# A three-layer edge network on one core: two gather pairs fewer, narrower node ranges, and nodes turned by the transposing form of the product

## The chip, the cores and the metric

The kernel runs on one core of a Trainium2 chip. The metric is the device time in microseconds of one execution; lower is better. TensorE (PE in the views), its weight loads (PEld), VectorE (DVE), ScalarE (ACT), GpSimd (POOL) and SyncE (SP) run side by side and meet at semaphores; 16 DMA engines move data.

## The reference

3125 nodes with 128 features, 53125 edges with 64 attributes, sorted by target `dst`. Three layers, then a last normalisation of `x` plus the result:

```python
for k in range(3):
    e = edge_vector @ edge_W[k] + edge_b[k]
    msg = relu(x[src] + e)
    agg = segment_sum(msg, dst, num_segments=n)
    z = (1.0 + eps[k]) * x + agg
    h = relu(batch_norm(z @ W1[k] + b1[k]))
    x = relu(layer_norm(h @ W2[k] + b2[k], ln_g, ln_b))
```

## The kernel before

**Bodies.** The edges are cut into 26 blocks of 2048 (16 tiles of 128 edges). Two blocks make a body, so there are 13 bodies, and each layer goes through all 13: 39 visits. A block is worked in four quads of four tiles. The first block of a body is called s, the second p.

**Two ways to fetch x[src].** The p block's rows come by indirect DMA: GpSimd issues four of them for each quad (`gather` of the gpsimd part, line 634), into `rows`. For quad q of the next body it waits until VectorE has added the rows of the present one (`p_added`). The s block is sorted by the remainder class of its source before the layers begin, so that each of its tiles needs only a few of 25 "slices" of the node table. `FIRST[t]` is the first slice that tile t may need and `SPAN[t]` how many. TensorE selects the rows (`gather`, lines 1499 to 1511): for each tile and slice, called a pair here, three bfloat16 products, one for each part of the table (x split in three, in `xs` and `xr`), with a one-hot matrix `hot_g` in float8 as weights. 68 pairs make 204 products a body, in quads of 48, 57, 54 and 45. The one-hots stand in `hot_g` by `RUNS`, 36 pairs for the first half of the tiles and 35 for the second; layer 0 builds them on VectorE (`build_hots`) and ScalarE (`last_hots`) and stores them, the later layers load them.

**Sum and scatter.** VectorE adds the gathered rows and the edge term: `add_s` (line 1167, from PSUM, waits for the gather's `g_filled`) and `add_p` (line 1174), in turns, one quad at a time. ScalarE applies the relu and widens the one-hots of the targets (`widen`, lines 731 and 733). TensorE then adds the messages into a PSUM bank by float32 products: `scatter_s` (line 1525) over `SORT_WINDOW` = 144 node columns that begin at the body's first target, `scatter_p` (line 1536) over `WINDOW` = 64 columns that begin at the quad's first target. Four products each a quad; the hardware records two weight loads and two products for each float32 product.

**Nodes.** From the third body on, each body also works two node tiles of 121 nodes of the layer's dense part: `transposed` (line 1545) turns the scaled x by a float32 product with the identity, then `hidden` (1552) and `output` (1558, 1560), with VectorE and ScalarE steps in between. The last four tiles come at the end of a layer.

**Staging.** Before the layers, 52 quads of edge attributes are multiplied by the weights of all three layers (lines 1491 and 1493), biased (1071), copied, scattered in sorted order and stored; VectorE also makes the targets' one-hots there (`hots_of`, line 1089), `HOT_COLS` = 416 words a quad, that is 104 KB, which every visit loads again (line 491).

**A branch for other data.** Before all this VectorE compares the edges with the windows and spans (`misfits`); edges that don't fit take a general loop, the `Else` branches.

**Order.** Each engine has its program written out by hand. In one visit TensorE runs: the turning of two node tiles, gather of quad 2, scatter of quad 0, gather 3, hidden, scatter 1, gather 0 of the next body, output, scatter 2, gather 1 of the next body, scatter 3.

Of the kernel before, what the change touches and what calls it, by code (L numbers as in the profile page):

```python
# [19 lines left out]
NODE_TILE = -(-NODES // BLOCKS)  # L20
NODE_TILES = BLOCKS
NODES_PAD = NODE_TILES * NODE_TILE
SORT_WINDOW = 144
WINDOW = 64
OVERLAP = BANK_COLS - NODE_TILE
GROUP = BANK_COLS // FEAT
GROUPS = -(-NODE_TILES // GROUP)
# [7 lines left out]
HALF = BLOCK_TILES // 2  # L35

FIRST = (0, 1, 2, 3, 5, 6, 8, 9, 11, 13, 14, 16, 17, 19, 21, 22)
SPAN = (3, 4, 4, 5, 4, 5, 5, 5, 5, 4, 5, 4, 5, 4, 3, 3)
SPANS = max(SPAN)

RUNS = (((0, 8), (0, 8), (0, 8), (1, 8), (3, 8)), ((8, 16), (8, 16), (8, 16), (8, 14), (8, 13)))
PAIRS_OF = [sum(b - a for a, b in runs) for runs in RUNS]
PAIRS = max(PAIRS_OF)
CHUNKS = ((0, 8), (8, 14), (14, SLICES))
# [2 lines left out]
SRT_COLS = LAYERS * FEAT + 2  # L47
HOT_COLS = QUAD * (SORT_WINDOW + WINDOW) // 2
EARLY_NODES = 20
# [20 lines left out]
def node(l, t):  # L70

    return l * NODE_TILES + t + 1


def pair_at(t, k):

    runs = RUNS[t // HALF]
    return sum(b - a for a, b in runs[:k]) + t - runs[k][0]


def constants():
# [5 lines left out]
    for s in range(SLICES):  # L87
        held = [t for t in range(BLOCK_TILES) if FIRST[t] <= s < FIRST[t] + SPAN[t]]
        c[:, C_LOW + s] = held[0] * P
# [6 lines left out]
def build(nc, x, attr, src, dst, dst_first, tabs, edge_w, edge_b, vecs, w1, w2, b2, ln_g, ln_b, tables, srt, ep, relrow, kept, hotrow, out):  # L96
# [3 lines left out]
    NT = NODE_TILE  # L100

    with ExitStack() as ctx:
        def sb(name, shape, dt=f32):
            return ctx.enter_context(nc.sbuf_tensor(name, shape, dt))

        def sem(name):
            return ctx.enter_context(nc.semaphore(name))
# [53 lines left out]
        ident = sb("ident", [P, P])  # L161
# [41 lines left out]
        relB = sb("relB", [P, 2, 2, HALF * P], f16)  # L203
        hot_s = sb("hot_s", [P, 2, QUAD * SORT_WINDOW])
        hot_p = sb("hot_p", [P, 2, QUAD * WINDOW])
        hot_stage = sb("hot_stage", [P, BLOCK_QUADS, HOT_COLS], bf16)
# [11 lines left out]
        def node_buffer(n):  # L218

            at = hot_words + n * TAIL * FEAT  # L220
            return region[:, at:at + TAIL * FEAT].rearrange("p (h d) -> p h d", h=TAIL)

        x_first = later[0:NT, 2 * QUAD * FEAT:2 * QUAD * FEAT + 4 * FEAT].rearrange("p (s h d) -> p s h d", s=2, h=2)
        x_eps, norm = node_buffer(0)[0:NT], node_buffer(1)[0:NT]
# [42 lines left out]
        def x_part(part, s):  # L267

            words = xr if part == 1 else xs
            return words[0:SLICE, :].bitcast(bf16)[:, 2 * s * FEAT + (part < 2):2 * (s + 1) * FEAT:2]  # L270
# [69 lines left out]
        xT_ready = sem("xT_ready")  # L340
# [39 lines left out]
        def wait_alone(eng, name, semaphore, value):  # L380

            eng.wait_ge(semaphore, value)
            eng.sem_inc(waits_passed[name], 1)
# [298 lines left out]
        def _(act):  # L682
# [43 lines left out]
            def widen(l, j, q):  # L726
# [3 lines left out]
                wait_alone(act, "act", s_done, l * LAYER_QUADS + j * BLOCK_QUADS + (q + BLOCK_QUADS - 1))  # L730
                nc.scalar.activation(hot_s[:, q % 2, :], packed[:, 0:QUAD * SORT_WINDOW], ACT.Copy).then_inc(hs_ready, 1)
                wait_alone(act, "act", p_done, l * LAYER_QUADS + j * BLOCK_QUADS + (q + BLOCK_QUADS - 1))
                nc.scalar.activation(hot_p[:, q % 2, :], packed[:, QUAD * SORT_WINDOW:], ACT.Copy).then_inc(hp_ready, 1)

# [5 lines left out]
            def last_hots(j, h):  # L740
# [9 lines left out]
                k = SPANS - 1  # L750
                a, b = RUNS[h][k]
                at, n = pair_at(a, k) * P, (b - a) * P
# [157 lines left out]
        def _(dve):  # L910
# [112 lines left out]
            for n, (limit, compare) in enumerate((  # L1023
                    (SORT_WINDOW, ALU.is_ge), (WINDOW, ALU.is_ge), (0, ALU.is_lt), (BANK_COLS - SORT_WINDOW, ALU.is_gt),
                    (BANK_COLS - WINDOW, ALU.is_gt), (0, ALU.is_lt), (0, ALU.is_lt), (0, ALU.is_gt))):
                ins = nc.vector.tensor_scalar(misfits[:, n:n + 1], ends[:, n:n + 1], float(limit), None, compare)
# [50 lines left out]
            def hots_of(g, first=0, stop=BLOCK_QUADS):  # L1077
# [5 lines left out]
                for at, window, relative in (  # L1083
                        (0, SORT_WINDOW, meta_s[:, g * BLOCK_TILES:(g + 1) * BLOCK_TILES, 1]),
                        (QUAD * SORT_WINDOW, WINDOW,
                         dst_rel[:, (2 * g + 1) * BLOCK_TILES:(2 * g + 2) * BLOCK_TILES])):
# [52 lines left out]
            def build_hots(j, h, first=0, stop=SPANS):  # L1139
# [9 lines left out]
                for k in range(first, stop):  # L1149
                    a, b = RUNS[h][k]  # L1150
                    at = pair_at(a, k) * P
# [314 lines left out]
        def _(pe):  # L1466
            for t in range(BLOCK_TILES):
                if t % QUAD == 0:
                    pe.wait_ge(one_ready, t // QUAD + 1)
                for b, weights in enumerate((tri, ones_b)):  # L1470
                    ins = nc.tensor.matmul(bank(b, BODIES * SLICES).rearrange("p (g s) -> p g s", s=SLICES), weights[:, :],
                                           one_s[:, t::BLOCK_TILES, :], start=t == 0, stop=t == BLOCK_TILES - 1,
                                           skip_group_check=True)
# [3 lines left out]
                             stop=True).then_inc(misfit_sum, 1)  # L1477
# [20 lines left out]
            def gather(l, j, q):  # L1498
# [6 lines left out]
                for t in range(q * QUAD, (q + 1) * QUAD):  # L1505
                    c = (t % QUAD) * FEAT
                    for k in range(SPAN[t]):
                        at = pair_at(t, k) * P
                        for part in range(3):
                            ins = nc.tensor.matmul(bank(q)[:, c:c + FEAT], hot_g[v % 2][0:SLICE, h, at:at + P],  # L1510
                                                   x_part(part, FIRST[t] + k), start=k == 0 and part == 0,
                                                   stop=k == SPAN[t] - 1 and part == 2, skip_group_check=True)
                ins.then_inc(g_filled, 1)
# [16 lines left out]
            def scatter_p(l, j, q, col):  # L1530
# [4 lines left out]
                for t in range(QUAD):  # L1535
                    ins = nc.tensor.matmul(ps[:, bass.ds(col, WINDOW)],  # L1536
                                           terms[:, BLOCK_QUADS + q, t * FEAT:(t + 1) * FEAT],
# [4 lines left out]
            def transposed(l, t, h, zh=zh_cols):  # L1542

                pe.wait_ge(x_eps_ready, node(l, t))
                nc.tensor.matmul(zh(h, 0), x_eps[:, h, :], ident[0:NT, 0:NT],  # L1545
                                 start=True, stop=True, skip_group_check=True).then_inc(xT_ready, 1)

            def hidden(l, t, h, upto, zh=zh_cols):

# [19 lines left out]
            def body(l, j):  # L1569
# [11 lines left out]
                if nodes:  # L1581
                    transposed(l, *a)
                    transposed(l, *b)
# [21 lines left out]
                if not last:  # L1605
                    gather(l, j + 1, 1)
                else:
                    pe.wait_ge(s_added, (l + 1) * LAYER_QUADS + BLOCK_QUADS)
                    for h in range(TAIL):
                        transposed(l, first + h, h, tail_zh)  # L1610
# [28 lines left out]
            with pe.Else():  # L1639
                pe.wait_ge(tables_ready, 1)  # L1640
                with pe.Fori(0, LAYERS) as l:

                    pe.wait_ge(x_eps_ready, l + 1)
                    for g, ts in enumerate(groups()):
                        for t in range(ts.start, ts.stop):
                            c = g * BANK_COLS + (t - ts.start) * NT
                            nc.tensor.matmul(ps[:, c:c + NT], result[:, t, :], ident[0:NT, 0:NT],
                                             start=t == ts.start, stop=False, skip_group_check=True)
                    with pe.Fori(0, BLOCKS) as b:
                        for k in range(BLOCK_QUADS):  # L1650
# [3 lines left out]
                            for j in range(QUAD):  # L1654
                                nc.tensor.matmul(bank(7)[:, j * FEAT:(j + 1) * FEAT], ones_b[0:B2_PARTS, :],
                                                 b2_split[:, bass.ds(l + LAYERS, 1), :].rearrange("p a d -> p (a d)"),
                                                 start=True, stop=False, skip_group_check=True)
                                ins = nc.tensor.matmul(bank(7)[:, j * FEAT:(j + 1) * FEAT],
                                                       g_attr[0:EDGE_FEAT, k, j * P:(j + 1) * P], one(we, l),
                                                       start=False, stop=True, skip_group_check=True)  # L1660
                            ins.then_inc(gg_filled, 1)
                            pe.wait_ge(g_msg, q + 1)
                            for j in range(QUAD):
                                for g in range(GROUPS):
                                    pe.wait_ge(g_hot, (q * QUAD + j) * GROUPS + (g + 1))
                                    nc.tensor.matmul(bank(g, GROUP_COLS), g_msgs[:, k % 2, j * FEAT:(j + 1) * FEAT],
                                                     onehot_all, start=False, stop=False,
                                                     skip_group_check=True).then_inc(g_used, 1)
# [5 lines left out]
                    for g, ts in enumerate(groups()):  # L1674
                        n = (ts.stop - ts.start) * NT
                        ins = nc.tensor.matmul(bank(g, n), w1_cur[:, :], zT_all[:, g * GROUP_COLS:g * GROUP_COLS + n],
                                               start=True, stop=True, skip_group_check=True)
                    ins.then_inc(g_step, 1)
                    wait_alone(pe, "pe", g_step, at + 3)
                    for g, ts in enumerate(groups()):  # L1680
# [3 lines left out]
                                         start=True, stop=False, skip_group_check=True)  # L1684
                        for t in range(ts.start, ts.stop):
                            c = g * BANK_COLS + (t - ts.start) * FEAT
                            ins = nc.tensor.matmul(ps[0:NT, c:c + FEAT], hT_all[:, t * NT:(t + 1) * NT], one(w2_all, l),
                                                   start=False, stop=t == ts.stop - 1, skip_group_check=True)
# [58 lines left out]
```

## Time and profile before

| | us |
|---|---|
| median of 3 runs | 1580.73 (1569.49 to 1582.17) |
| profiled execution, its own time | 1595.68 |
| its span, first to last instruction | 1593.9 |
| mean granted TensorE clock (1 is 2.4 GHz) | 0.862 |
| staging, to the first gather on TensorE | about 335 |
| three layers and the last normalisation | about 1259 |

The profiled execution is 15 us, or 0.9%, over the median. Busy shares of the span: PE 75%, PEld 65%, DVE 45%, ACT 35%, POOL 53%. A time of a row is the start in us from the span's beginning; "busy" of a group is the union of its instructions' times, while the mean of one is its own latency, and matmuls overlap: the step from one start to the next is what a further product costs. "issue" as a releaser stands for idle time whose end nothing in the trace explains; "remote" in the views of this single core is a semaphore whose sender the trace doesn't find.

### The profile page before, as it was taken

To read this page: it belongs to the slowest core of one execution; us is meant where nothing else is said; L and a number is where in the kernel's file an instruction comes from. 1 tells how busy PE (TensorE), PEld (TensorE's weight loads), DVE (VectorE), ACT (ScalarE), POOL (GpSimd) and SP (SyncE) were. 2 spreads that over 40 slices of the span, in tenths; PEclk is the share of its full clock that TensorE was granted. 3 is DMA by queue.
4 is the path that set the end of the run, shared out by engine and by line. 5 is a ranking of instruction groups with operands and counts; after the bars stand their busy time and mean duration, and the time that the engine had idled before them with its cause. 6 is when DMAs were issued, how large, how long until landed. Compare 5 with 4: busy or idle time off the path is not lost.

```text
span 1593.9 us, 31830 instructions
## 1 busy us (share of the span) xinstructions
PE 1200.5 (75%) x11868; PEld 1030.8 (65%) x11868; DVE 719.3 (45%) x1546; ACT 551.4 (35%) x1146; POOL 839.7 (53%) x842
## 2 busy tenths in 40 slices
PE   4666656666888878886588888788856888888886
PEld 2333323355778778776477877777845777787776
DVE  7576456564454454455122333233351244344345
ACT  1223323233444444442233333333422333333333
POOL 6777667756555454432555545544155445445440
PEclk8879888787988898987798998889967899988987
DMA  9999999995565656556355555555634555555541
GB/s 240 324 320 352 298 337 344 325 297 174 177 184 169 183 166 184 179 178 195 88 174 144 169 170 156 165 150 158 186 100 139 173 162 152 175 160 166 171 136 52
DMA packets 252723, 309.79 MB, mean 194 GB/s; under 512 B 53005, under 2 KB 169791, under 8 KB 252583
## 3 DMA queue, kind: packets, MB, share of 16 engines
q1 hardware_dynamic: 208734, 218.79, 44.8%
q0 software_dynamic: 33280, 82.06, 16.2%
q10 hardware_dynamic: 10569, 6.97, 1.9%
q8 instruction: 100, 1.64, 0.4%
q14 instruction: 40, 0.33, 0.1%
HBM read 200.17 MB, written 107.55 MB: 193 GB/s over the span
## 4 chain that ended last, share of the span: by engine, by line
PE 64%; issue 19%; DVE 8%; another core or an unknown queue 5%; DMA 2%; ACT 1%; SPq 1%; DVEq 0%; ACTq 0%
PE ps L1510 33%; PE ps L1525 11%; PE ps L1536 9%; PE ps L1491 5%; DVE terms L1071 2%; PE ps L1560 2%; DMA ep_dram<-terms 2%; PE ps L1545 1%; PE ps L1552 1%; PE ps L1558 1%; DVE hot_stage L1089 1%; PE ps L1493 1%; ACT region L711 1%; DMA attr_x<-attr_dram 1%
## 5 line engine op out<-in xcount | busy, mean ns | idle before, releaser
L634 POOL DMA_INDIRECT rows<-table_dram,src_i x416 | 402.1, 967 | 440.2 <-DVE terms L1174 256.2
L1167 DVE TENSOR_TENSOR terms<-ps,terms 128x512 f32<-128x512 f32 x156 | 107.8, 691 | 667.3 <-PE ps L1510 333.5
L1510 PE MATMUL ps<-xs,early_words 125*128 125x128 bf16 x2720 | 292.1, 230 | 82.2 <-issue 73.0
L1510 PE MATMUL ps<-xs,region 125*128 125x128 bf16 x2584 | 271.1, 230 | 53.2 <-issue 52.9
L634 POOL DMA_INDIRECT rows<-x_dram,src_i x208 | 211.9, 1019 | 175.4 <-DVE terms L1174 121.4
L1510 PEld LDWEIGHTS ps<-xs,early_words 125*128 125x128 fp8e4 x2720 | 231.8, 103 | 99.0 <-issue 89.2
L1510 PE MATMUL ps<-xr,early_words 125*128 125x128 bf16 x1360 | 265.2, 230 | 35.5 <-issue 35.2
L1491 PE MATMUL ps<-wf,attr_x 64*128 64x384 f32 x416 | 187.5, 603 | 112.9 <-issue 61.5
L654 POOL DMA_INDIRECT srt_dram<-region,pos_i x208 | 223.5, 1075 | 88.8 <-issue 59.1
L1510 PE MATMUL ps<-xr,region 125*128 125x128 bf16 x1292 | 250.7, 230 | 17.3 <-issue 17.2
L1510 PEld LDWEIGHTS ps<-xs,region 125*128 125x128 fp8e4 x2584 | 220.7, 103 | 59.7 <-issue 59.5
L1525 PE MATMUL ps<-hot_s,terms 128*128 128x144 f32 x1248 | 213.4, 316 | 21.0 <-issue 19.0
L1491 PEld LDWEIGHTS ps<-wf,attr_x 64*128 64x128 f32 x416 | 91.3, 232 | 196.4 <-issue 170.6
L718 ACT ACTIVATE terms<-terms 128x512 f32<-128x512 f32 x156 | 97.6, 625 | 340.2 <-DVE terms L1167 304.2
L1525 PEld LDWEIGHTS ps<-hot_s,terms 128*128 128x128 f32 x1248 | 185.5, 212 | 30.9 <-issue 30.6
L1536 PE MATMUL ps<-hot_p,terms 128*128 128x64 f32 x1248 | 178.2, 284 | 23.8 <-issue 22.8
L1536 PEld LDWEIGHTS ps<-hot_p,terms 128*128 128x128 f32 x1248 | 170.2, 206 | 34.7 <-issue 34.2
L1493 PE MATMUL ps<-wf,attr_x 64*128 64x384 f32 x416 | 188.8, 606 | 0.0
L1510 PEld LDWEIGHTS ps<-xr,early_words 125*128 125x128 fp8e4 x1360 | 138.5, 102 | 46.0 <-issue 45.7
L711 ACT ACTIVATE region<-ps 128x768 f32<-128x768 f32 x104 | 84.0, 811 | 214.4 <-PE ps L1491 86.5
L1071 DVE TENSOR_TENSOR terms<-ps,eb_all 128x768 f32<-128x768 f32 x104 | 96.9, 953 | 125.7 <-remote 38.9
L1510 PEld LDWEIGHTS ps<-xr,region 125*128 125x128 fp8e4 x1292 | 132.3, 102 | 25.8 <-issue 25.2
(129 smaller groups left out, 1315.8 us busy)
## 6 DMA issues: line engine op xcount, KB each, us to landing
ep_dram<-terms SPq DMA_DIRECT2D x52, 768.0 KB
terms<-srt_dram SPq DMA_DIRECT2D x156, 256.0 KB
terms<-ep_dram SPq DMA_DIRECT2D x156, 256.0 KB
early_words<-hotrow_dram SPq DMA_DIRECT2D x156, 104.0 KB
attr_x<-attr_dram SPq DMA_DIRECT2D x52, 256.0 KB
region<-kept_dram SPq DMA_DIRECT2D x13, 576.0 KB
early_words<-kept_dram SPq DMA_DIRECT2D x13, 576.0 KB
region<-kept_dram SPq DMA_DIRECT2D x13, 560.0 KB
```

What stands on the lines that cost most here:

```text
L634: pool.indirect_dma_start(rows[:, q, t * FEAT:(t + 1) * FEAT], None, source, bass.IndirectOffsetOnAxis(ap=src_i[:, c:c + 1], axis=0),).the ...
L654: pool.indirect_dma_start(srt, bass.IndirectOffsetOnAxis(ap=pos_i[:, c:c + 1], axis=0), stage_s[:, q, t, :], None).then_inc(scattered[q], 16)
L711: nc.scalar.activation(stage_s[:, q, tiles, 0:LAYERS * FEAT], ps[:, 0:QUAD * BANK_COLS].rearrange("p (t c) -> p t c", t=QUAD) [:, tiles, 0 ...
L718: nc.scalar.activation(terms[:, q, :], terms[:, q, :], ACT.Relu).then_inc(s_relu, 1)
L1071: nc.vector.tensor_tensor(stage_p[:, n % 2, :].rearrange("p (l t d) -> p t l d", l=LAYERS, t=QUAD)[:, tiles], ps[:, BLOCK_QUADS * BANK_COL ...
L1167: nc.vector.tensor_tensor(terms[:, q, :], bank(q), terms[:, q, :], ALU.add).then_inc(s_added, 1)
L1491: of_s = nc.tensor.matmul(bank(t, width), attr_x[0:EDGE_FEAT, slot, cut], wf[0:EDGE_FEAT, :], start=True, stop=True, skip_group_check=True)
L1493: of_p = nc.tensor.matmul(bank(BLOCK_QUADS + t, width), attr_x[EDGE_FEAT:P, slot, cut], wf[EDGE_FEAT:P, :], start=True, stop=True, skip_gr ...
L1510: ins = nc.tensor.matmul(bank(q)[:, c:c + FEAT], hot_g[v % 2][0:SLICE, h, at:at + P], x_part(part, FIRST[t] + k), start=k == 0 and part == ...
L1525: ins = nc.tensor.matmul(ps[:, bass.ds(col, SORT_WINDOW)], terms[:, q, t * FEAT:(t + 1) * FEAT], hot_s[:, q % 2, t * SORT_WINDOW:(t + 1) * ...
L1536: ins = nc.tensor.matmul(ps[:, bass.ds(col, WINDOW)], terms[:, BLOCK_QUADS + q, t * FEAT:(t + 1) * FEAT], hot_p[:, q % 2, t * WINDOW:(t + ...
L1560: nc.tensor.matmul(y(h), hT[:, h, :], w2_all[:, l, :], start=False, stop=True, skip_group_check=True).then_inc(y_ready, 1)
```

## The change

Four constants and one call. Tile 1 loses its fourth slice and tile 6 its fifth; the pair of tile 1 also goes from the stored one-hots (36 to 35 pairs), that of tile 6 stays stored and isn't used. The target windows shrink from 144 to 132 and from 64 to 48 columns, and with them `HOT_COLS` from 416 to 360. The two nodes' turning uses the engine's transposing form.

```diff
-SORT_WINDOW = 144
-WINDOW = 64
+SORT_WINDOW = 132
+WINDOW = 48
...
-SPAN = (3, 4, 4, 5, 4, 5, 5, 5, 5, 4, 5, 4, 5, 4, 3, 3)
+SPAN = (3, 3, 4, 5, 4, 5, 4, 5, 5, 4, 5, 4, 5, 4, 3, 3)
...
-RUNS = (((0, 8), (0, 8), (0, 8), (1, 8), (3, 8)), ((8, 16), (8, 16), (8, 16), (8, 14), (8, 13)))
+RUNS = (((0, 8), (0, 8), (0, 8), (2, 8), (3, 8)), ((8, 16), (8, 16), (8, 16), (8, 14), (8, 13)))
...
             def transposed(l, t, h, zh=zh_cols):
 
                 pe.wait_ge(x_eps_ready, node(l, t))
-                nc.tensor.matmul(zh(h, 0), x_eps[:, h, :], ident[0:NT, 0:NT],
-                                 start=True, stop=True, skip_group_check=True).then_inc(xT_ready, 1)
+                nc.tensor.transpose(zh(h, 0), x_eps[:, h, :], ident[0:NT, 0:NT]).then_inc(xT_ready, 1)
```

On TensorE, where a visit of layer 0 ends with the scatter of quad 3 and the next begins by turning two node tiles (`region` holds them; `col_i` is the window's column), the program had:

```order
L1525 MATMUL ps<-hot_s,terms 128x144 x4
L1576 TENSOR_LOAD col_i
L1576 ISA x2
L1536 ISA
L1536 MATMUL ps<-hot_p,terms 128x64 x4
L1545 MATMUL ps<-ident,region 128x121 x2
```

In the changed kernel the same place reads:

```order
L1525 MATMUL ps<-hot_s,terms 128x132 x4
L1575 TENSOR_LOAD col_i
L1575 ISA x2
L1536 ISA
L1536 MATMUL ps<-hot_p,terms 128x48 x4
L1545 MATMUL ps<-ident,region 128x121 x2
```

Nothing moved there: the same instructions stand in the same order, with fewer columns. The gathers between such places are 6 products shorter a body (quad 0 from 48 to 45, quad 1 from 57 to 54), 234 in all.

On VectorE, in the staging, the one-hots of the targets (`hot_stage`) are made between the bias additions (`terms`). A piece of the difference:

```order
-L1089 TENSOR_TENSOR hot_stage<-iota_f,meta_s 128x576
-L1089 TENSOR_TENSOR hot_stage<-iota_f,dst_rel 128x256
+L1089 TENSOR_TENSOR hot_stage<-iota_f,meta_s 128x528
+L1089 TENSOR_TENSOR hot_stage<-iota_f,dst_rel 128x192
 L1071 TENSOR_TENSOR terms<-ps,eb_all 128x2x3x128 x2
```

Again only the sizes differ. VectorE has 1537 instructions in its program before and after.

## Rows read from the trace of the kernel before

**Rows 1.** The page: granted TensorE clock in 40 slices, in tenths.
```profile
PEclk8879888787988898987798998889967899988987
```
**Rows 2.** Stretch: us, busy PE, PEld, DVE, ACT, POOL, PEclk, DMA share, GB/s.
```profile
0.00:335.00 335.00, 196.31 (x871) 108.97 (x872) 203.82 (x276) 91.20 (x159) 239.95 (x233) 0.83 0.97 319
335.00:1594.00 1259.00, 1004.23 (x11000) 921.85 (x10997) 515.43 (x1271) 460.15 (x987) 599.80 (x610) 0.87 0.55 161
```
**Rows 3.** The chain that ended last, 335 to 1594 us, shares by line.
```profile
by line: PE ps L1510 41.2%; issue 19.6%; PE ps L1525 13.9%; PE ps L1536 11.3%; another core or an unknown queue 2.8%; PE ps L1560 2.7%; PE ps L1545 1.8%; PE ps L1552 1.5%; PE ps L1558 1.2%; DVE terms L1174 0.4%; DVE region L1213 0.3%; DVE s
```
**Rows 4.** Timeline of PE at 2.4 GHz: start, us, line, tiles, count.
```profile
905.58 1.15 PE L1525 MATMUL ps<-hot_s,terms 128*128 128x144 f32 x8
906.57 1.00 PE L1536 MATMUL ps<-hot_p,terms 128*128 128x64 f32 x8
907.41 0.22 PE L1510 MATMUL ps<-xs,early_words 125*128 125x128 bf16 x1
907.47 0.22 PE L1510 MATMUL ps<-xr,early_words 125*128 125x128 bf16 x1
...
926.49 0.66 PE L1545 MATMUL ps<-ident,region 121*128 121x121 f32 x4
926.98 0.22 PE L1510 MATMUL ps<-xs,early_words 125*128 125x128 bf16 x1
```
**Rows 5.** Timeline of PE at 1.2 GHz, two places.
```profile
904.81 0.31 PE L1510 MATMUL ps<-xr,region 125*128 125x128 bf16 x1
904.92 0.31 PE L1510 MATMUL ps<-xs,region 125*128 125x128 bf16 x1
...
977.28 2.12 PE L1525 MATMUL ps<-hot_s,terms 128*128 128x144 f32 x8
979.20 1.50 PE L1536 MATMUL ps<-hot_p,terms 128*128 128x64 f32 x8
```
**Rows 6.** PE inside one gather, idle time and its releaser in brackets.
```profile
914.99 0.22 PE L1510 MATMUL ps<-xr,early_words 125*128 125x128 bf16 x1 [0.52 <-issue]
916.40 0.22 PE L1510 MATMUL ps<-xs,early_words 125*128 125x128 bf16 x1 [1.19 <-issue]
```
**Rows 7.** Who waited for whom, from 335 us: total, times, longest.
```profile
PE ps L1510 <- issue: 178.3, 255, 12.1
POOL rows L634 <- DVE terms L1174: 377.6, 115, 8.6
DVE terms L1167 <- PE ps L1510: 333.5, 71, 17.4
DVE terms L1167 <- remote: 330.9, 71, 13.0
```
**Rows 8.** Timeline of POOL, one burst of four issues and the next's first.
```profile
1000.38 0.94 POOL L634 DMA_INDIRECT rows<-table_dram,src_i  x1 [2.66 <-DVE terms L1174]
...
1004.12 0.94 POOL L634 DMA_INDIRECT rows<-table_dram,src_i  x1 [0.30 <-issue]
1007.65 0.94 POOL L634 DMA_INDIRECT rows<-table_dram,src_i  x1 [2.59 <-DVE terms L1174]
```
**Rows 9.** Timeline of DVE around the same burst.
```profile
1006.09 0.69 DVE L1167 TENSOR_TENSOR terms<-ps,terms 128x512 f32<-128x512 f32 x1 [5.98 <-remote]
1006.70 0.68 DVE L1174 TENSOR_TENSOR terms<-rows,terms 128x512 f32<-128x512 f32 x1
```
**Rows 10.** Busy time by stretch: a single burst, a double one, two layer ends.
```profile
1000.38:1007.65 7.27, 6.89 (x91) 6.39 (x88) 1.50 (x3) 1.33 (x3) 3.77 (x4) 1.00 0.41 123
...
1022.30:1037.10 14.80, 9.66 (x92) 8.15 (x90) 2.73 (x5) 4.17 (x9) 7.60 (x9) 0.81 0.55 158
...
702.60:744.80 42.20, 32.96 (x314) 29.93 (x313) 20.91 (x68) 17.72 (x45) 0.03 (x1) 0.82 0.71 217
1545.00:1582.50 37.50, 34.52 (x312) 31.40 (x311) 21.41 (x74) 15.19 (x38) 0.00 (x0) 0.82 0.22 58
```
**Rows 11.** The chain in the staging, 25 to 335 us, shares by line.
```profile
by line: PE ps L1491 26.2%; issue 16.9%; another core or an unknown queue 12.7%; DVE terms L1071 11.5%; DMA ep_dram<-terms 8.1%; DVE hot_stage L1089 4.4%; PE ps L1493 3.2%; ACT region L711 2.9%; DMA attr_x<-attr_dram 2.9%; SPq L461 2.0%; DV
```

## The prediction

> **What bounds the kernel now.** I read the busy time by stretch first. Staging takes 335 us with the DMA engines 97% busy; the layers take 1259 us with PE busy for 1004, POOL for 600 and DMA 55% [rows 2]. Almost all that the change touches is in the layers, on PE. The chain of waits says the same: 41.2% of the 1259 us lies on the gather (L1510), 13.9% on scatter_s (L1525), 11.3% on scatter_p (L1536), 1.8% on the turning (L1545), and 19.6% is "issue", idle time that nothing explains [rows 3]. On that view alone PE is the bound and each PE nanosecond saved counts.
>
> The timeline speaks against taking that whole. Inside a gather, where no product waits for a semaphore, PE runs one product and stops for 0.52 or 1.19 us [rows 6]; in the gathers such and other "issue" idling sums to 178 us in 255 pieces [rows 7]. I laid these stops beside POOL. GpSimd issues its indirect DMAs in bursts of four: 0.94 us each, about 1.25 apart, so 1000.38 to 1005.06. VectorE's next add_s starts at 1006.09, a microsecond behind the burst, add_p at 1006.70, and the next burst at 1007.65 [rows 8, 9]. In steady stretches this repeats every 7.3 us: a burst of 4.7 us and 2.6 us between. Within a burst PE gets through some 50 to 60 products, and stops until about 0.9 us after its end; the semaphores that PE should have raised arrive then too, which is why half of VectorE's waits for the gather are put down to "remote" (330.9 us beside 333.5) [rows 7]. So there is a loop POOL burst, PE's late signal, add_s, add_p, POOL burst, whose period holds little that the change shortens. In one period PE started 91 products [rows 10]; a quad needs 70 (204 gather, 64 scatter and 14 node products, over four). So PE gets ahead, VectorE then adds two quads at once, and a burst of eight follows in which PE manages 92 products in 14.8 us [rows 10] and falls behind again. Of POOL's waits for VectorE, 115 with 377.6 us together [rows 7], 115 times 2.6 = 299 us is the loop's own minimum, and the other 79 us is time in which PE really is late.
>
> **The change part by part.** The sum is made against the profiled execution (span 1593.9, own time 1595.68), which is 15 us over the median of 1580.73; I take the difference over to the median unchanged.
>
> *Gather.* 39 visits times 6 products = 234 of 7956 go. A product more costs 0.06 us at 2.4 GHz (907.41 to 907.47) [rows 4] and 0.11 at 1.2 GHz (904.81 to 904.92) [rows 5]. The chain has 0.412 x 1259 / 7956 = 65 ns for one, a mix of both clocks: 234 x 65 ns = 15 us. Bounds: 13 us with no slow stretch among them, 25 with nothing else. The Trainium skill, "TensorE: Matmul & The Clock Gate", section "Back-to-back issue gap", gives about 81 ns for a weight load and product of 128 columns in a stream; by it this term would be an estimated 19 us. The trace has 57, and the row decides.
>
> *scatter_s, 144 to 132 columns.* Eight recorded products take 0.99 us at 2.4 GHz (905.58 to 906.57), 124 ns each [rows 4], and 1.92 us at 1.2 GHz, 240 each [rows 5]: exactly two passes of 144 columns at 1.2 GHz. Two passes of 132 are 10 ns shorter at 2.4 and 20 at 1.2 GHz; with a mean clock of 0.87, 1248 products give 14 us. Below, the saving could be cut off where the weight load sets the step; the rows of scatter_p put that at 105 ns, under the 114 that I expect. Bounds 4 us (a straight line from 64 columns and 105 ns to 144 and 124) and 15 us (13.9% of 1259, times 12/144).
>
> *scatter_p, 64 to 48 columns.* Eight take 0.84 us (906.57 to 907.41), 105 ns each; four products of the turning, of 121 columns, take 0.49 us, 122 each [rows 4]. Nearly twice the columns for 17 ns more: at these widths the weights of 128 columns, not the moving columns, set the step. So nothing is gained. Bounds: 0, and if it did go with the columns 11.3% of 1259 times 16/64 = 36 us, which the comparison all but excludes.
>
> *Turning.* 78 products, each four-way split now into two weight loads and two products: 0.49 us for two of them, 0.245 each [rows 4]. No transposing form is in this trace. Bounds: nothing gained (the same two passes), or 0.245 down to one bfloat16 step of 0.06, 14 us for all. I take one recorded pair in place of two, 0.12 us, 9 us in all, because the operand's width stays 4 bytes.
>
> *Not on the path.* The widening on ScalarE and the one-hot loads shrink by 13%; ScalarE is busy for 460 of 1259 us and DMA 55% [rows 2], so PE's gather in between hides them. If that cover were gone they would gain, not cost. Nothing is added, no wait is new. That the narrower windows fit follows from the reference's edges: the farthest target is 124 columns from its body's first (under 132) and 33 from its quad's (under 48), and the general branch isn't taken.
>
> *Staging.* VectorE's one-hots are 4.4% of the chain of 310 us [rows 11], 13.6 us, and lose 13.5% of their elements: 2 us.
>
> *The sum.* PE saves 15 + 14 + 0 + 9 = 38 us if it always is the path. The three layer ends, after POOL's last burst, hold about 950 of the 11000 products (314 and 312 in the two shown [rows 10]), 9%: there 3.5 us count in full. Of the other 34.5 us I count half. For it speaks that PE, once behind in a double burst, has to catch up through several quads, so that its savings add up until the next wait; against it that 299 of 378 us of POOL's waits are the loop's minimum. So 3.5 + 17 + 2 = 23 us. Span 1571, profiled 1573, median **1558 us**, 1.4% faster.
>
> **The rivals.**
>
> 1. *PE is the bound throughout.* The chain's shares speak for it. Then all 38 us count, the stops shrink with the number of products (2.9% of 178 us, 5 us), and staging 2: 45 us, 1536 us. The loop's regular 7.3 us speak against it.
>
> 2. *POOL's loop absorbs it.* PE gets earlier to a stop that ends with the burst anyway. Then the layer ends and staging are left, 5.5 us, and a little of the 79 us: 5 to 12 us, 1572 us. For it: 299 of the 378 us in which POOL waits are not due to PE being late. Against it: every double burst shows PE behind for two to three quads.
>
> 3. *The clock takes it back; slower.* PEclk falls in nearly every slice [rows 1], and 1 - 0.862, doubled, of 1594 us is 440 us at 1.2 GHz. It falls after stretches in which PE stands: the double burst has 0.81, the single one 1.00 [rows 10]. Shorter work between the same bursts means longer standing. A microsecond more at 1.2 GHz costs half a microsecond of PE work, and half of that on the path. The gain of 23 us is gone once 92 us more are spent there, a fifth over now; at a third over (147 us, 37 us lost) the time is 1595 us. Since only some 1 us in 30 a visit is freed, I hold that unlikely. The Trainium skill has a rule against the turning here (the same page, Part 4, "PE-mode transpose"): transposing products don't count as work for the clock. No row of before has one. By it the quiet time would grow by a quarter of a microsecond twice in a visit, in 33 of the visits.
>
> 4. *The turning gains nothing and scatter_s takes its lower bound.* PE saves 15 + 4, half of it counts: 12 to 13 us, 1568 us.
>
> **How the numbers follow.** Forecast 0.42 (1548 to 1567), rival 1 0.16 (1530 to 1548), rival 2 0.26 (1567 to 1578), rival 3 0.08 (1581 to 1600), rival 4 0.08. From 1536 to 1580 I leave out rival 3 and half of rival 1: about 2 in 10. About 1% is what a measurement of this kernel can tell from no change (its three runs span 0.8%), so faster is below 1565 and slower above 1597. Faster: rival 1 with most of the forecast and a part of rival 4, 0.53. Slower: the far half of rival 3 and what I haven't seen, 0.07. The rest, 0.40, is within 1%.
>
> **What would show it.** The gather has 7722 products, the scatters 1248 each; at 2.4 GHz eight of scatter_s take 0.91 us, eight of scatter_p still 0.84. If these go down to 0.63, the weights didn't set the step. The turning has 78 recorded products, not 156. POOL's steady period stays at 7.3 us; if it stays and the total of POOL's waits for VectorE falls from 378 by some 20 us, the forecast's halving is right; if those waits hardly move, rival 2. A mean clock under 0.84 speaks for rival 3. The staging ends 2 us sooner. Wrong altogether I would be if the stops in the gathers change in kind, since their cause is not known: they are 178 us, far more than all that is saved.

## The result, and the profile after

The changed kernel takes 1589.05 us (median of 20 runs, 1573.84 to 1603.92), the kernel before beside it 1581.05 (20 runs, 1569.49 to 1596.3): ratio 1.0044, 95% interval 1.0022 to 1.0065. It is 7 us slower, within 1% of before; forecast were 23 us less. A second comparison, side by side with others on one chip, gave 1.0055 (1.0020 to 1.0091). A third, on a chip where the kernel before itself takes only 1223 us, gave 0.9812 (0.9777 to 0.9847), 23 us less. The explanation needs both kinds of chip. Ratios leave out runs more than 1.5% above the fastest of their kernel; in the second comparison that is 14 of before's 29, and the plain medians there (1600.84 and 1597.78) give 1.0019, so that slowdown is known only as 0.2 to 0.6%.

TensorE's rows came out as the sum had them. Timeline of PE in the changed kernel, at 2.4 GHz, then at 1.2, then the turning (start, us, line, tiles, count), beside [rows 4, 5]:

```profile
556.97 1.07 PE L1525 MATMUL ps<-hot_s,terms 128*128 128x132 f32 x8
557.88 0.99 PE L1536 MATMUL ps<-hot_p,terms 128*128 128x48 f32 x8
558.70 0.22 PE L1510 MATMUL ps<-xs,region 125*128 125x128 bf16 x1
...
436.50 1.96 PE L1525 MATMUL ps<-hot_s,terms 128*128 128x132 f32 x8
438.26 1.13 PE L1536 MATMUL ps<-hot_p,terms 128*128 128x48 f32 x8
...
595.66 0.39 PE L1545 MATMUL ps<-ident,region 121*128 121x121 f32 x2
595.89 0.22 PE L1510 MATMUL ps<-xs,early_words 125*128 125x128 bf16 x1
```

Eight products of scatter_s take 0.91 us in place of 0.99 and 1.76 at 1.2 GHz in place of 1.92; eight of scatter_p 0.82 in place of 0.84; two turnings, now one recorded product each, 0.23 in place of 0.49. What changed elsewhere shows in the busy time by stretch (us, busy PE, PEld, DVE, ACT, POOL, PEclk, DMA share, GB/s), to be read beside [rows 2]:

```profile
0.00:335.00 335.00, 207.08 (x876) 111.19 (x877) 199.54 (x276) 90.62 (x160) 236.68 (x231) 0.78 0.95 315
335.00:1579.00 1244.00, 984.27 (x10683) 903.84 (x10680) 512.26 (x1271) 444.50 (x987) 599.68 (x611) 0.85 0.55 161
```

PEclk is lower in both stretches, 0.78 for 0.83 and 0.85 for 0.87; over 20 runs the mean granted clock is 0.837 (standard error 0.001), where before has 0.858 to 0.862 in the comparisons below that take as long. The staging's fall isn't the change's doing as far as this shows: PE's work there is the same, and the profiles of the experiments on such chips have anything from 0.79 to 0.84 there. It makes up about a third of the gap between these two profiles (0.832 for 0.862), which is why the clocks below are means over many runs. The waits of the layers, beside [rows 7] (total, times, longest):

```profile
POOL rows L634 <- DVE terms L1174: 383.1, 116, 8.0
...
DVE terms L1167 <- PE ps L1510: 396.1, 85, 17.7
...
DVE terms L1167 <- remote: 252.1, 57, 9.5
...
PE ps L1510 <- issue: 179.8, 259, 12.0
```

POOL waits 383 us for VectorE, as before (378); PE stops for 180 us inside the gathers, as before (178). The profiled execution happens to be one of the shortest of the 20 (1580.81), so its span is no measure of the change.

### The profile page after: what moved, and what is told of

Read it like the earlier page. It is cut to its first block, busy times and chain, and to the rows that moved or that the text cites. A ratio compares the mean times of both kernels' runs of the same rounds, so it can differ in the third digit from the quotient of the medians.

```text
span 1579.0 us, 31206 instructions
## 1 busy us (share of the span) xinstructions
PE 1191.3 (75%) x11556; PEld 1015.0 (64%) x11556; DVE 711.8 (45%) x1546; ACT 535.1 (34%) x1146; POOL 836.4 (53%) x842
## 4 chain that ended last, share of the span: by engine, by line
PE 66%; issue 19%; DVE 7%; DMA 4%; another core or an unknown queue 2%; SPq 1%; ACT 0%; ACTq 0%; DVEq 0%
PE ps L1510 34%; PE ps L1525 11%; PE ps L1536 10%; PE ps L1491 6%; DMA ep_dram<-terms 4%; DVE terms L1071 2%; PE ps L1559 2%; PE ps L1551 1%; PE ps L1557 1%; PE ps L1493 1%; PE ps L1545 1%; DVE hot_stage L1089 0%; DVE xr L947 0%; DVE z_sum L993 0%
## 5 line engine op out<-in xcount | busy, mean ns | idle before, releaser
L1510 PE MATMUL ps<-xs,early_words 125*128 125x128 bf16 x2640 | 287.1, 233 | 69.2 <-issue 65.5
L1491 PE MATMUL ps<-wf,attr_x 64*128 64x384 f32 x416 | 197.2, 626 | 108.1 <-issue 57.4
L1525 PE MATMUL ps<-hot_s,terms 128*128 128x132 f32 x1248 | 204.4, 308 | 29.6 <-issue 28.2
L1525 PEld LDWEIGHTS ps<-hot_s,terms 128*128 128x128 f32 x1248 | 177.9, 213 | 43.1 <-issue 42.5
L1536 PE MATMUL ps<-hot_p,terms 128*128 128x48 f32 x1248 | 183.2, 289 | 26.8 <-issue 24.8
L1493 PE MATMUL ps<-wf,attr_x 64*128 64x384 f32 x416 | 198.6, 630 | 0.0
L1536 PEld LDWEIGHTS ps<-hot_p,terms 128*128 128x128 f32 x1248 | 177.0, 215 | 33.4 <-issue 32.2
```

Of the source, the lines that this page charges most:

```text
L1491: of_s = nc.tensor.matmul(bank(t, width), attr_x[0:EDGE_FEAT, slot, cut], wf[0:EDGE_FEAT, :], start=True, stop=True, skip_group_check=True)
L1493: of_p = nc.tensor.matmul(bank(BLOCK_QUADS + t, width), attr_x[EDGE_FEAT:P, slot, cut], wf[EDGE_FEAT:P, :], start=True, stop=True, skip_gr ...
L1525: ins = nc.tensor.matmul(ps[:, bass.ds(col, SORT_WINDOW)], terms[:, q, t * FEAT:(t + 1) * FEAT], hot_s[:, q % 2, t * SORT_WINDOW:(t + 1) * ...
L1536: ins = nc.tensor.matmul(ps[:, bass.ds(col, WINDOW)], terms[:, BLOCK_QUADS + q, t * FEAT:(t + 1) * FEAT], hot_p[:, q % 2, t * WINDOW:(t + ...
```

## The experiments

Each ratio is to the kernel before, run beside it on the same chip; the clocks are means over the runs of each kernel. The expectations name the accounts that were set against each other: theory A, that the clock follows what PE streams while it is occupied, and the rivals B to F.

### One part at a time

Four kernels, each the kernel before with one edit of the change: `SPAN` and `RUNS`; the transposing form; and

```diff
-WINDOW = 64
+WINDOW = 48
```

```diff
-SORT_WINDOW = 144
+SORT_WINDOW = 132
```

Pairs: 

> Only the two gather pairs are left out: 234 products fewer, windows and turning as before. The changed kernel took a mean granted clock of 0.832 where before had 0.862. Theory A (the clock falls because products stream fewer columns in steps that do not get shorter; here columns and steps go together): clock within 0.005 of before, time 5 to 12 us less (ratio 0.993 to 0.997). Rival B (any shortening of PE's work lengthens its standing behind GpSimd's bursts, and that lowers the clock): clock 0.85 or less, time within 3 us of before.

Turning: 

> Only the turning uses the transposing form: 78 recorded products in place of 156. Theory A: the transposed products stream less in the same place; a small fall of the clock, 0.855 or so, time within 3 us. Rival C (transposing products do not count for the clock, and they are what lowers it in the changed kernel): clock 0.84 or less, time 5 to 15 us more. Rival B: no change that can be seen, since only some 9 us of PE's work go.

scatter_p: 

> Only scatter_p's range goes from 64 to 48 columns. In the changed kernel eight of its products still take what they took before, so the engine is occupied as long and streams a quarter less. Theory A: clock 0.845 or less, time 8 to 16 us more (ratio 1.005 to 1.010). Rival B: nothing gets shorter, so clock 0.86 and time within 3 us of before.

scatter_s: 

> Only scatter_s's range goes from 144 to 132 columns; its step falls from 124 to 113 ns with it. Theory A: columns and time go together, clock within 0.006 of before, time 3 to 8 us less. Rival B: 14 us of PE's work go, PE stands that much longer, clock 0.85, time as before.

| alone | ratio (95%) | clock, before 0.858 |
|---|---|---|
| pairs left out | 1.0003 (0.9967 to 1.0039) | 0.850 |
| turning | 0.9961 (0.9933 to 0.9989) | 0.857 |
| scatter_p 48 | 1.0035 (1.0009 to 1.0060) | 0.850 |
| scatter_s 132 | 1.0010 (0.9982 to 1.0038) | 0.852 |

(Standard errors of the clocks 0.001 to 0.002, 12 runs each, 35 of before.) Theory A was right on the direction of scatter_p: it occupies PE as long, streams a quarter less, the clock falls and the kernel gets slower. The size was smaller than it wanted (0.850 for 0.845 or less, 0.35% for 0.5 to 1%). On the pairs and scatter_s it wanted a clock within 0.005 and 0.006 of before, and both fell further, by 0.008 and 0.007. Those two save 15 and 14 us of PE's work and show no gain clear of the noise. That is what rival B said of them, that PE's longer standing lowers the clock, and no run here parts it from the fewer columns in these two; but it has no account of scatter_p, which shortens nothing. Rival C falls: the turning is the one edit with a gain clear of the noise, and its clock is unchanged. The four falls sum to 0.024, and the changed kernel lies 0.02 to 0.03 under before.

### Giving columns back

The changed kernel with 64 columns in scatter_p, and the kernel before with 96 (`WINDOW = 64` and `WINDOW = 96`).

> The changed kernel with scatter_p's range put back to 64 columns. So far, apart: pairs -1.7 us with the clock 0.008 lower, scatter_s +2.1 us and 0.007 lower, turning -5.0 us and 0.001 lower, scatter_p +5.9 us and 0.008 lower than before's 0.858. If the parts add up (theory A, the clock follows what the array streams): clock 0.842, time 5 us less than before (ratio 0.997), that is 6 us under the changed kernel. Rival (the parts do not add; the changed kernel is slow by something they do only together): clock about 0.837 and ratio 1.003 or more as in the changed kernel.

Measured 0.9951 (0.9917 to 0.9984), 1573.71 us beside 1585.14, clock 0.855 (before 0.862). **This kernel is faster than before, and by its ratio faster than the changed one.** Alone 48 columns cost 0.35%; in company of the others about 0.9%.

> Kernel before with scatter_p's range widened to 96 columns: 80 thousand more column passes of products, whose step should stay at 105 ns since two passes of 96 columns are 80 ns at 2.4 GHz; the one-hot loads grow from 104 to 120 KB a quad. Theory A: clock up by 0.012 to 0.018, to 0.872, and time down by 8 to 12 us (ratio 0.993 to 0.995), the reverse of the narrower range. Rival D (the narrower range costs time for another reason than the clock, or more columns only cost): clock unchanged, time equal or up to 10 us more from larger loads.

Measured 1.0008 (0.9978 to 1.0039), clock 0.869: up by 0.006, less than expected, and no time gained. The loads and the widening also grew, so this run doesn't say whether they ate the gain or the higher clock brought none.

To part the streamed columns from the one-hots' size, the changed kernel kept its 48 columns in every store, load and widening, and only the products streamed more, over zeros set once. From the edit (ScalarE also writes its 48 columns into places 64 or 96 apart):

```diff
-        hot_p = sb("hot_p", [P, 2, QUAD * WINDOW])
+        hot_p = sb("hot_p", [P, 2, QUAD * STREAM])
...
-                    ins = nc.tensor.matmul(ps[:, bass.ds(col, WINDOW)],
+                    ins = nc.tensor.matmul(ps[:, bass.ds(col, STREAM)],
```

> The changed kernel itself once more, as the yardstick for the three beside it on one chip: ratio 1.002 to 1.007, clock 0.02 under before.

> The changed kernel, scatter_p's one-hots made, stored, loaded and widened with 48 columns, but each product streams 64: the 16 further columns of hot_p were set to zero once and add nothing. With true 64-column one-hots the kernel was 0.5% faster than before, with 48 it is 0.4% slower. Theory A (what counts is how many columns the products stream, by way of the clock): clock up by 0.01 to 0.02 over the changed kernel and ratio to before 0.993 to 0.998, as with true 64 columns. Rival F (the narrower one-hots cost by their loads, their layout or ScalarE's widening): clock and ratio as in the changed kernel, 1.002 or more.

> The same with 96 columns streamed, 48 of them zero. Eight products still take 0.84 us at 2.4 GHz, since two passes of 96 columns are 80 ns and the step is 105. Theory A: clock up once more, 0.005 to 0.015 over the stream of 64, time equal to that or up to 5 us less. In the kernel before, true 96 columns raised the clock by 0.006 and left the time as it was, so the gain may already be used up at 64. Rival F: as the changed kernel.

| on one chip, before 1597.78 us | median us | ratio (95%) | clock, before 0.859 |
|---|---|---|---|
| changed kernel | 1600.84 | 1.0055 (1.0020 to 1.0091) | 0.830 |
| 48, 64 streamed | 1585.03 | 0.9959 (0.9926 to 0.9993) | 0.848 |
| 48, 96 streamed | 1587.88 | 0.9984 (0.9946 to 1.0022) | 0.858 |

Streaming 16 columns of zeros makes the kernel 16 us faster. That shows it: the loads, the stored layout and ScalarE's work are the changed kernel's (rival F; ScalarE's widening of `hot_p` takes 356 and 355 ns), the order of instructions too, and only what the array streams differs. The profiled executions show by what way. The layers' stretch and the wait inside the gathers, first with 48 streamed, then with 64:

```profile
337.00:1609.00 1272.00, 1013.11 (x10688) 932.76 (x10688) 513.68 (x1272) 445.79 (x987) 597.37 (x610) 0.83 0.54 157
PE ps L1510 <- issue: 174.3, 246, 12.7
...
343.00:1594.00 1251.00, 975.21 (x10688) 892.81 (x10686) 513.57 (x1272) 445.62 (x987) 599.12 (x612) 0.86 0.55 160
PE ps L1513 <- issue: 185.8, 253, 13.0
```

PE has as many products and is busy for 38 us less at the higher clock, while its stops are no shorter (186 us for 174). In these two executions the time comes by the clock and not by the stops. At 96 the clock is before's and no further time comes; beyond 64 it bought nothing here.

### What GpSimd's bursts take

GpSimd issues one indirect DMA a quad after the first visit, not four. The rows of three tiles in four stay as they were, so VectorE adds old values, and its wait counts the fewer landings; all else runs. The edit takes away the issues together with their transfers.

```diff
             def gather(l, source, j, q):
 
-                for t in range(QUAD):
+                for t in range(QUAD if (l, j) == (0, 0) else 1):
```

> Kernel before, but GpSimd issues one indirect DMA a quad in place of four, except for the first visit: the rows of the other three tiles of a quad are not fetched again and stay as they were. Bursts of 1 us in place of 5. Theory of the forecast (PE's stops inside gathers come from GpSimd's bursts): the 178 us of 'issue' in the gathers fall under 60, and the time falls by 150 to 350 us. Rival E (the stops are PE's own, of its instruction supply or clock): 'issue' in the gathers stays at 150 or more and the time falls by less than 60 us.

> The changed kernel with the same cut on GpSimd (one indirect DMA a quad in place of four, the other rows stay as they were). Theory of the forecast (the loop of bursts absorbed the savings): now PE is the bound, so this is 35 to 45 us faster than the same cut of the kernel before. Theory A (the clock takes the savings back, with or without the loop): less than 20 us faster, at a clock lower by 0.015 or more.

> The changed kernel with 64 columns in scatter_p and GpSimd's issues cut to one indirect DMA a quad (the rows of three tiles in four stay as they were from the first visit). With 48 columns and the same cut it took 1191 us at a clock of 0.923. If 48 columns cost time only by way of PE's stops and the clock that falls in them: 1191 within 3 us, and the clock within 0.003. If the narrower range costs or saves PE time by itself: 5 us or more to one side.

Kernel before, cut: 1229.54 us, ratio 0.775 (0.7704 to 0.7796), 356 us less. Changed kernel, cut: 1191.35 us. The waits and the layers' stretch of the cut kernel before:

```profile
POOL rows L634 <- DVE terms L1174: 602.0, 141, 9.9
DVE terms L1167 <- PE ps L1510: 313.3, 143, 3.9
...
PE ps L1510 <- issue: 25.0, 6, 11.5
...
DVE terms L1167 <- remote: 0.7, 1, 0.7
```

```profile
335.00:1228.00 893.00, 845.11 (x10963) 824.53 (x10960) 510.16 (x1269) 454.57 (x986) 150.79 (x154) 0.97 0.65 194
```

The stops in the gathers are gone (25 us in 6 pieces for 178 in 255), the late semaphores too ("remote" 0.7 us for 331), the layers' PEclk is 0.97 for 0.87, and PE is busy for 845 of 893 us. Rival E falls. Whether it is the issuing or the transfers that stop PE, this run can't say. With PE the bound, the change is worth 38.2 us (four runs of each), against the 38 of the sum. Theory A's wording for this pair, that the clock takes the savings back with or without the loop, falls with it: the clocks are 0.923 and 0.925. With 64 columns in scatter_p the cut kernel has the ratio 0.7528 (0.7470 to 0.7585), with 48 it had 0.7524 (0.7481 to 0.7568), on another chip: no cost of 48 columns is seen, in intervals of about 0.5% to either side, too wide to exclude one of 0.35%. Its time, 1198.25 us, lay outside the 1191 within 3 us that were expected, beside a before that was 13 us slower as well.

### Two chips without the stops

The next kernels fell on a chip on which the kernel before took 1223.21 us. The first streams the old 144 columns in scatter_s too, by the same edit on `hot_s`; the others cut GpSimd's issues to two a quad (`else 2`), so that two tiles' rows in four stay as they were.

> The changed kernel with one-hots of 132 and 48 columns, but products that stream 144 and 64 (the rest zero), as before did: PE saves only the gather pairs and half the turning, 24 us of work. If the clock takes the larger part of the gain (theory A): clock 0.855 or more and ratio to before 0.996 or less, as good as or better than the stream of 132 and 64 (0.9959) in spite of 14 us more of PE work. If the bursts absorb it and the clock is minor: ratio 0.997 to 1.000.

> Kernel before with two indirect DMAs a quad in place of four (two tiles' rows in four stay as they were): bursts of 2.2 us. With one it took 1229 us. If PE's stops begin only after it has worked through some 50 products within a burst, which takes it over 3 us, they are nearly gone here too: 1230 to 1260 us, 'issue' in the gathers under 60 us. If GpSimd slows PE in proportion to its activity: about 1350 us.

> The changed kernel with the same cut to two. If stops are nearly gone: 33 to 40 us faster than the same cut of the kernel before, as with one issue (38). If half of the stops are left: 10 to 25 us.

| without stops | median us | ratio to the uncut kernel before |
|---|---|---|
| streams of 144 and 64 | 1205.63 | 0.9853 (0.9833 to 0.9873) |
| kernel before, two issues | 1209.89 | 0.9879 (0.9855 to 0.9905) |
| changed kernel, two issues | 1173.18 | 0.9576 (0.9549 to 0.9603) |

There were no stops here to begin with, so none of the three answers its question; the pair still shows 36.7 us between the two kernels once GpSimd's issues are halved. Three more fell on another such chip:

> The changed kernel. On a chip where before takes about 1223 us (no stops, clock 0.93) PE's saved 38 us should all count: ratio 0.965 to 0.975. On a chip where it takes 1580 to 1600 us: 1.002 to 1.008, as twice before.

> One-hots of 132 and 48 columns, products that stream 144 and 64. Without stops: 0.985 as measured. With stops: if the clock takes the larger part of the gain, 0.996 or less at a clock of 0.855 or more; if the bursts absorb it and the clock is minor, 0.997 to 1.000.

> The changed kernel with 64 columns in scatter_p. Without stops: the same as the changed kernel within 0.003, since scatter_p's step is set by its weights and the clock hardly falls there. With stops: 0.993 to 0.997, 0.8% under the changed kernel.

| without stops, before 1223.49 us | median us | ratio (95%) | clock, before 0.933 |
|---|---|---|---|
| changed kernel | 1197.98 | 0.9812 (0.9777 to 0.9847) | 0.924 |
| streams of 144 and 64 | 1206.06 | 0.9859 (0.9835 to 0.9883) | 0.928 |
| 64 columns in scatter_p | 1200.45 | 0.9826 (0.9807 to 0.9845) | 0.923 |

The waits of the changed kernel here, its layers' stretch, and POOL's timeline:

```profile
DVE terms L1167 <- PE ps L1510: 250.1, 112, 6.1
POOL rows L634 <- issue: 228.5, 585, 28.0
...
PE ps L1510 <- issue: 24.7, 4, 12.9
POOL rows L634 <- DVE terms L1174: 14.2, 23, 7.5
```

```profile
302.00:1196.00 894.00, 826.01 (x10712) 799.72 (x10708) 517.80 (x1279) 440.83 (x992) 618.50 (x619) 0.95 0.76 229
```

```profile
702.92 0.94 POOL L634 DMA_INDIRECT rows<-table_dram,src_i  x1 [0.31 <-issue]
704.17 0.94 POOL L634 DMA_INDIRECT rows<-table_dram,src_i  x1 [0.30 <-issue]
705.42 0.94 POOL L634 DMA_INDIRECT rows<-table_dram,src_i  x1 [0.30 <-issue]
```

GpSimd issues every 1.25 us without a pause here, four issues a quad as ever, and PE runs on beside it. POOL hardly waits for VectorE (14 us for 383). And the chain of the same execution names the new bound:

```profile
by line: POOL rows L634 29.3%; PE ps L1510 24.8%; issue 16.1%; PE ps L1525 8.0%; PE ps L1536 7.3%; DMA rows<-table_dram,src_i 2.2%; PE ps L1559 2.0%; DMA ep_dram<-terms 1.5%; PE ps L1551 1.2%; PE ps L1557 0.9%; PE ps L1545 0.7%; DMA rows<-x
```

624 issues at 1.25 us are 780 of the layers' 894 us. That fits that of PE's 38 us only 23 arrive, and 36.7 where GpSimd's issues are halved: the expectation of 0.965 to 0.975 was too good since it took PE for the bound, and GpSimd is nearly one. Streaming the old columns costs here (0.9859 for 0.9812), and the clock rises by no more than 0.004. Giving scatter_p its 64 columns back changes nothing, as expected (0.9826, clock 0.923): where nothing stops PE, the 48 columns have no price.

## Why the prediction was wrong, point by point

*The terms of the sum.* As PE's own work all held. Gather: 234 products fewer. scatter_s: 10 ns a product at 2.4 GHz and 20 at 1.2. scatter_p: no gain, its weights set the step. Turning: 0.115 us a product in place of 0.245. Together 38 us forecast; 38.2 and 36.7 measured where GpSimd's issues are cut.

*The staging.* 2 us were forecast; the first gather starts at 334.2 us for 334.7. Nothing to be told from one execution of each.

*The loop of bursts.* Its effect was right: GpSimd's bursts stop PE, and the stops go with the bursts. The first step that failed is its share. I let half of 34.5 us count, plus 3.5 at the layer ends and 2 in the staging. With scatter_p's columns given back, the gain on a chip with stops is 0.49% or 8 us (0.9951; 11 us by the plain medians), of PE's same 38 us: a fifth to three tenths, not six tenths. The clock is 0.007 lower there and may have taken a part. But with 96 columns streamed it is before's (0.858 for 0.859), PE's saving is still some 34 us (the step is 0.108 us for 0.105), and the gain is 3 us (0.9984; 10 us by the plain medians), where half would be 17. The prediction's own sign said as much: if POOL's waits for VectorE hardly moved, rival 2. They were to fall from 378 by some 20 us and were 383, with 7.5 us from the start of one burst of four to the next (median) in both traces. Rival 2's 5 to 12 us is what the change brings without scatter_p's narrower range.

*The clock.* The second step that failed, and the one that made the change a loss, is the claim that scatter_p's narrower range is worth nothing either way, and with it the weight of rival 3: the term stood at 0 and measured 16 us the wrong way in company of the others. Of the 23 us, then, some 15 never arrive behind the bursts, and 16 go with scatter_p's columns: 8 us slower. Rival 3 had the place and the clock, under 0.84. Its size agrees too, 92 us more at 1.2 GHz to eat 23 us: on one chip the clock goes from 0.859 to 0.830, so the time at 1.2 GHz from 2 x 0.141 x 1597 = 450 us to 2 x 0.170 x 1601 = 544 us, 94 us more. That is in part luck, since not all of the 23 us were there to be eaten. And I argued it from the wrong cause. I looked for longer standing and saw only 1 us in 30 freed; what the runs show is that how much the array streams while it is occupied counts, in scatter_p without any shortening at all. That has a price that a sum of durations doesn't contain. I gave it 0.08.

*The rule on transposing products.* The Trainium skill, "TensorE: Matmul & The Clock Gate", Part 4, "PE-mode transpose", says that transposing products don't count as work for the clock. Turning alone had a clock of 0.857 beside 0.858 and was 0.4% faster; with 78 such products in 11000, no run here shows the rule, and none needs it.

*The profile as evidence.* The forecast was laid on one execution of before with all stops in it. On two chips the same program takes 1223 us, and the traces taken there of the changed kernel have no such stops (none was kept of the kernel before). Nothing in the first trace could tell that its largest loss isn't there everywhere.

*Open.* Why PE is stopped behind GpSimd's bursts on some chips and not on others (each was met once, so it may be something other than the chip); how the loss between PE's 38 us and the 8 that arrive divides between loop and clock (the kernel with both old streams met only chips without stops); whether the pairs and scatter_s lower the clock by their columns or by PE's longer standing; why 48 columns cost more beside the other edits than alone; and why columns beyond 64 raise the clock and bring no time.

## What to carry to other kernels

An edit that makes products narrower where the weights set the step saves nothing, and where PE is stopped again and again and its clock swings between 1.2 and 2.4 GHz it can cost (16 us here, nothing on a chip without stops): look for the granted clock beside each saving, and compare it over many runs, where it was a sharper measure than the time. When an engine stops inside a run of instructions that wait for nothing, cut the suspected neighbour's work to see what the stops cost before costing small edits; here they were 356 us beside the 38 that were saved. And measure on more than one chip before a ratio under 1% is believed: this change was 0.2 to 0.6% slower in two comparisons and 1.9% faster in a third.

## What the runs showed of the hardware

- GpSimd's indirect DMAs in bursts of four let PE start some 50 to 60 products, then stop it until a microsecond behind the burst, on some chips; a burst of one leaves no stops there. On two other chips bursts without end left none.
- Sixteen more columns of zeros in each of 1248 products raised the mean granted clock from 0.830 to 0.848 and took 16 us off, on a chip with these stops. In a kernel without them the clock and the time were the same at 48 and 64 (0.924 and 0.923; 1197.98 and 1200.45 us).
- Float32 products with weights of 128 columns cost nearly the same at 48, 64 and 96 columns at 2.4 GHz (0.103, 0.105 and 0.108 us a recorded product, by the shortest eight in a row); 132 cost 0.113, 144 cost 0.122. At 1.2 GHz it is 0.197, 0.199 and 0.206.
- The transposing form of a float32 product of 121 columns is one recorded load and product, 0.115 us for 0.245.
